# A routed-expert kernel: the table of slots holds whole token rows, so that an expert's rows come by one plain load

## The reference

```
gu = x @ shared_gate_up_w
shared = silu(gu[:, :512]) * gu[:, 512:] @ shared_down_w ; shared *= sigmoid(x @ shared_gate_w)
w, idx = top_k(softmax(x @ gate_w), 8) ; w /= sum(w)
pos  = running count of the tokens sent to this expert so far
slot = min(pos, 128)                       # capacity 128; later tokens are dropped
buf[expert, slot] = x[token]
out_e = (silu(buf @ gate_w[e]) * (buf @ up_w[e])) @ down_w[e]
y[token] += w * out_e[expert, slot]        # only where pos < 128
```

## Time and profile before

| What | Value |
|---|---|
| Median of three runs | 1972.29 us |
| The profiled execution's own time | 1962.54 us |
| Its span | 1960.8 us |
| PE busy | 1706.9 us (87%) |
| DVE busy | 1329.0 us (68%) |
| ACT busy | 971.5 us (50%) |
| POOL busy | 1068.3 us (54%) |
| DMA, mean over the span | 41 GB/s, 80.15 MB |
| Chain that ended last | PE 55%, issue 15%, DVE 14%, ACT 7%, POOL 4%, DMA 3% |

### The profile page before, as it was taken

The page is one execution under the profiler, slowest core; times in us unless marked ns, Lnnn a source line. Parts: engine busy times, 40 slices in busy tenths (PEclk is TensorE's granted clock), DMA queues, the critical chain, the costliest instruction groups (busy, mean ns, idle before and its releaser), DMA issues.

```text
span 1960.8 us, 51981 instructions
## 1 busy us (share of the span) xinstructions
PE 1706.9 (87%) x17309; PEld 1427.6 (73%) x17309; DVE 1329.0 (68%) x4615; ACT 971.5 (50%) x2803; POOL 1068.3 (54%) x1772
## 2 busy tenths in 40 slices
PE   3799999989899998999999999999999986457665
PEld 2687887878788887788878888888888864246554
DVE  5477777767677776677777777777777764335564
ACT  2365555555455554555555555555555543123332
POOL 2115555555455555555555555555555543568897
PEclk8899999999999999999999999999999997678999
DMA  4001100000000101000000000000000000147887
GB/s 126 8 14 21 21 19 19 19 14 19 19 19 19 19 19 19 19 19 19 17 16 19 19 19 19 19 19 19 19 19 19 18 13 13 45 124 186 199 205 154
DMA packets 97568, 80.15 MB, mean 41 GB/s; under 512 B 33835, under 2 KB 95224, under 8 KB 97528
## 3 DMA queue, kind: packets, MB, share of 16 engines
q1 hardware_dynamic: 68856, 60.46, 11.2%
q0 software_dynamic: 28672, 19.18, 5.5%
HBM read 51.63 MB, written 27.95 MB: 41 GB/s over the span
## 4 chain that ended last, share of the span: by engine, by line
PE 55%; issue 15%; DVE 14%; ACT 7%; POOL 4%; DMA 3%; another core or an unknown queue 1%; POOLq 0%; SPq 0%; DVEq 0%; ACTq 0%
PE bank L1055 15%; PE bank L964 7%; PE ps_m L964 5%; ACT p L787 3%; PE ps_lg L1113 3%; PE ps_yo L1069 3%; PE ps_lg L964 3%; PE ps_tr L986 3%; PE ps_yo L964 3%; PE ps_pt L1128 2%; PE bank L1041 2%; DMA xg<-xrows,gid 2%; PE ps_pt L964 1%; DVE rmax L1599 1%; PE ps_lg L1020 1%
## 5 line engine op out<-in xcount | busy, mean ns | idle before, releaser
L574 POOL DMA_INDIRECT table<-toki,slot x512 | 520.2, 1016 | 242.5 <-issue 196.3
L518 POOL TENSOR_TENSOR pool_pad<-pad_in 128x1 f32<-128x1 f32 x456 | 115.7, 254 | 400.8 <-PE ps_lg L1113 176.6
L787 ACT ACTIVATE p<-ps_lg,rmax 128x77 f32<-128x77 f32 x1024 | 235.6, 349 | 146.8 <-DVE rmax L1599 141.6
L1055 PE MATMUL bank<-h_h,wb 128*128 128x256 f16 x2048 | 266.3, 273 | 4.3 <-issue 2.2
L1055 PE MATMUL bank<-h_l,wb 128*128 128x256 f16 x2048 | 266.3, 273 | 0.0
L1055 PEld LDWEIGHTS bank<-h_l,wb 128*128 128x128 f16 x2048 | 200.8, 98 | 23.8 <-issue 0.2
L1055 PEld LDWEIGHTS bank<-h_h,wb 128*128 128x128 f16 x2048 | 193.2, 98 | 28.3 <-issue 2.8
L590 POOL TENSOR_TENSOR rs<-nt,minushalf 128x2 f32<-128x2 f32 x128 | 92.6, 724 | 188.2 <-DVE nt L1503 176.7
L1534 DVE SCALAR_TENSOR_TENSOR h_l<-bank,h_h 128x512 f16<-128x512 f32 x256 | 174.8, 683 | 12.0 <-ACT h_h L768 6.7
L1599 DVE TENSOR_REDUCE rmax<-ps_lg 128x8 f32<-128x616 f32 x128 | 101.6, 794 | 84.9 <-PE ps_lg L1113 84.8
L773 ACT ACTIVATE h_h<-bank 128x512 f16<-128x512 f32 x128 | 76.9, 601 | 124.3 <-PE bank L1055 124.3
(11 more groups left out here) (287 smaller groups left out, 4691.6 us busy)
## 6 DMA issues: line engine op xcount, KB each, us to landing
ew<-in_egu_w SPq DMA_DIRECT2D x64, 256.0 KB
xrows<-xr SPq DMA_DIRECT2D x32, 320.0 KB
x<-in_x SPq DMA_DIRECT2D x32, 256.0 KB
out<-x SPq DMA_DIRECT2D x32, 256.0 KB
table<-toki,slot POOLq DMA_INDIRECT x512
ew<-in_edown_w SPq DMA_DIRECT2D x64, 128.0 KB
ctx<-in_ctxT SPq DMA_DIRECT2D x32, 77.0 KB, 2.0
stage_b<-in_k SPq DMA_DIRECT2D x1, 1024.0 KB, 8.0
```

Source lines behind the costliest of these rows:

```text
L518: return g.tensor_tensor(pool_pad[:, site:site + 1], pad_in[:, :], pad_in[:, :], ALU.mult)
L574: g.indirect_dma_start(out=table, out_offset=bass.IndirectOffsetOnAxis(ap=slot[:, t, k:k + 1], axis=0), in_=toki[:, t:t + 1], in_offset=No ...
L787: ins = a.activation(p32[:, h * S2:(h + 1) * S2], ps_lg[:, h // HB, h % HB * S2:(h % HB + 1) * S2], ACT.Exp, bias=rmax[r % 2][:, h:h + 1])
L1055: ins = mm(two(bank[j % 2])[:, m % 2, :], wb1[:, k, m * P:(m + 1) * P], hp[:, k, :], start=(i == 0 and k == 0), stop=(i == 1 and k == FK - 1))
```

## The change

A table slot now holds a whole row of 321 float32 values (`TW`): the 320 of `xr` and the token's number. The array `xrows` is gone.

- **Batch loop.** In place of `store_rows`, SyncE copies `xr` to a second SBUF tile `xs` (`pass_rows`, 320 KB, SBUF to SBUF). That copy first waits until all scatters of the batches before have landed. VectorE writes the token's number into column 320 of `xs`. Each of the 16 scatters of a batch writes 128 rows of 1284 bytes from `xs` instead of 128 numbers of 4 bytes. Group "a" also waits for the copy.
- **Start.** The sentinel table of 32 KB is replaced by eight DMAs (`clear_table`), each of 1024 rows of 1284 bytes, 10.5 MB in all, placed behind `load_x(1)` in SyncE's order. GpSimd waits for them before its first scatter.
- **Between the loops.** Loading the table, its float copies, its transposition and `ids` are gone.
- **Expert loop.** SyncE loads an expert's 128 rows of the table with one plain DMA (`load_rows`), ahead of the expert's weights, four experts ahead. The gathers on GpSimd and the `gid` copies on VectorE are gone, with one of the two `plain`. `ids_across` is one float32 product of the last column of `xg` with the identity in place of two float16 products.

```diff
-            def store_rows(b):
+            def pass_rows(b):
                 sp.wait_ge(ch_ok, b + 1)
                 sp.wait_ge(ln_nm[3], b + 1)
-                sp.dma_start(xrows[bass.ds(b * S, S)].rearrange("(t p) n -> p t n", p=P), xr[:, :, :]).then_inc(xr_out, 16)
+                w(sp, scattered, 16 * T2 * TOPK * b)
+                sp.dma_start(xs[:, :, 0:XR], xr[:, :, :]).then_inc(xr_out, 16)
...
-            sp.wait_ge(consts, 1)
-            sp.dma_start(table.rearrange("(e c) o -> e (c o)", c=CAP), sent[:, :]).then_inc(table_dma, 16)
+            def clear_table(es):
+                sp.dma_start(table[es.start * CAP:es.stop * CAP].rearrange("(e c) n -> c e n", c=CAP),
+                             xg[1][:, :].unsqueeze(1).to_broadcast([P, len(es), TW])).then_inc(table_dma, 16)
...
             load_x(1)
+            for k in range(0, E, E // 8):
+                clear_table(range(k, k + E // 8))
             load_ctx(2)
             load_x(2)
...
-            def load_slots():
-                sp.wait_ge(scattered, 16 * T2 * TOPK * NB)
-                sp.dma_start(slots_row[:, :], table.rearrange("(e c) o -> e (c o)", c=CAP)).then_inc(table_dma, 16)
+            def load_rows(e, u):
+                w(sp, e_wt, e - XD + 1)
+                w(sp, e_aid, e - XD + 1)
+                w(sp, e_same, e - XD + 1)
+                sp.dma_start(xg[u][:, :], table[bass.ds(e * CAP, CAP)]).then_inc(e_x[u], 16)
+            def load_expert(e, u):
+                load_rows(e, u)
+                load_weights(e, u)
...
                 if group == "a":
                     pool.wait_ge(slots_ok, b + 1)
                     pool.wait_ge(tok_ok, b + 1)
+                    pool.wait_ge(xr_out, 16 * b + 16)
...
-                        in_=toki[:, t:t + 1], in_offset=None, bounds_check=NT - 1, oob_is_err=False,
+                        in_=xs[:, t, :], in_offset=None, bounds_check=NT - 1, oob_is_err=False,
...
-            def gather(e, u):
-                pool.wait_ge(e_gid, e + 1)
-                w(pool, e_tr, e - XD + 1)
-                w(pool, e_wt, e - XD + 1)
...
-                g.indirect_dma_start(
-                    out=xg[u][:, :], out_offset=None, in_=xrows,
-                    in_offset=bass.IndirectOffsetOnAxis(ap=gid[u][:, 0:1], axis=0),
-                    bounds_check=NT - 1, oob_is_err=False).then_inc(e_x[u], 16)
...
-                for half in (slots_h, slots_l):
-                    ins = mm(ps_row[:, 0:CAP], ident16[:, bass.ds(e, 1)].to_broadcast([P, P]), half[:, :],
-                             start=(half is slots_h), stop=(half is slots_l))
-                ins.then_inc(e_row, 1)
+                mm(ps_row[:, 0:CAP], xg[u][:, XR:TW].to_broadcast([P, P]), ident[:, :], start=True, stop=True).then_inc(e_row, 1)
```

More of the change, by code:

```diff
@@ L31 @@
 XR = D + E
+TW = XR + 1
 EPS = 1e-5
@@ L93, in build @@
 def build(nc, x, ctxT, maskT, g_xattn, g_ffn, wq0, wk0, wv0, bq0, bk0, bv0, k0, k1, k2, s0, s1, s2,
-          wqT1, wkvT1, wcT1, gates_w, sgu_w, sdown_w, egu_w, edown_w, out, xrows, table):
+          wqT1, wkvT1, wcT1, gates_w, sgu_w, sdown_w, egu_w, edown_w, out, table):
     es = ExitStack()
@@ L223, in build @@
         xr = sb("xr", [P, T2, XR])
+        xs = sb("xs", [P, T2, TW])
         th = sb("th", [P, IS // P, S])
@@ L245, in build @@
         x4 = sb("x4", [P, T2, D])
[L247 to L252, removed]
         aid = [sb(f"aid{i}", [P, 1], I32) for i in range(XD)]
-        xg = [sb(f"xg{i}", [P, XR]) for i in range(XD)]
+        xg = [sb(f"xg{i}", [P, TW]) for i in range(XD)]
         ew = [sb(f"ew{i}", [P, 3, D]) for i in range(XD)]
@@ L309, in build @@
         e_x, e_out = sems("e_x", XD), sems("e_out", 2)
-        ids_f, ids_t, e_gid, e_aid = (sem(n) for n in ("ids_f", "ids_t", "e_gid", "e_aid"))
+        e_aid = sem("e_aid")
         e_tr, e_eg, e_gu, e_th, e_ga, e_ac, e_dn, e_wt, e_y0 = (
@@ L433, in _ @@
             store_x4(0)
-            store_rows(0)
+            pass_rows(0)
             load_ctx(4)
@@ L438, in _ @@
                 store_x4(n - 2)
-                store_rows(n - 2)
+                pass_rows(n - 2)
                 load_ctx(n + 2)
@@ L443, in _ @@
                 store_x4(b)
-                store_rows(b)
-            store_rows(NB - 1)
+                pass_rows(b)
+            pass_rows(NB - 1)
             def load_weights(e, u):
@@ L458, in _ @@
             store_x4(NB - 1)
-            load_slots()
-            each_expert(sp, load_weights, XD)
+            sp.wait_ge(scattered, 16 * T2 * TOPK * NB)
+            for e in range(XD):
+                load_rows(e, e)
+            each_expert(sp, load_expert, XD)
             for par in range(2):
@@ L508, in _ @@
             for rows in xg:
-                g.memset(rows[:, :], 0.0).then_inc(consts2, 1)
+                g.memset(rows[:, 0:XR], 0.0).then_inc(consts2, 1)
+            g.memset(xg[1][:, XR:TW], float(NT)).then_inc(consts2, 1)
             g.memset(vc2[:, :, :], 0.0).then_inc(consts2, 1)
@@ L642, in _ @@
                 body(n)
-            pool.wait_ge(table_dma, 16 * 4)
+            pool.wait_ge(table_dma, 16 * 11)
             body(2)
@@ L683, in add_out @@
                     compute_op=ALU.add).then_inc(e_out[u % 2], 16)
-            g.memset(pool_pad[:, 3:5], 0.0).then_inc(pad_ok, 2)
-            for e in range(XD - 1):
-                gather(e, e)
+            g.memset(pool_pad[:, 4:5], 0.0).then_inc(pad_ok, 1)
             pool.wait_ge(x4_out, 16 * NB)
@@ L691, in step @@
                 if not isinstance(e, int):
-                    pool.wait_ge(pad_ok, 2 * (e - 2 * XD + 1))
-                if within(e, XD - 1):
-                    gather(e + XD - 1, (u - 1) % XD)
+                    pool.wait_ge(pad_ok, e - 2 * XD + 1)
                 if within(e, -1):
@@ L1337, in last_batch @@
                 d_dn(1, b)
-            pe.wait_ge(consts2, 30)
+            pe.wait_ge(consts2, 31)
             pe.wait_ge(setup_lo, 5)
@@ L1828, in _ @@
             from_bools(1)
-            dve.wait_ge(consts2, 30)
+            dve.wait_ge(consts2, 31)
             body(-1)
@@ L1865, in match @@
                 w(dve, e_cr, e - 2)
-                v.tensor_scalar(same[u % 2][:, :], ps_row[:, 0:CAP], idsf[:, bass.ds(e - 1, 1)], None, ALU.is_equal).then_inc(e_same, 1)
+                v.tensor_scalar(same[u % 2][:, :], ps_row[:, 0:CAP], xg[(u - 1) % XD][:, XR:TW], None, ALU.is_equal).then_inc(e_same, 1)
             def weight(e, u):
@@ L1905, in expert @@
                     summed(e - 1, (u - 1) % XD)
-            for e in range(XD - 1):
-                gather_ids(e, e)
             weight(0, 0)
@@ L1941 @@
     out = nc.dram_tensor("out_0", [NT + 3 * CAP, D], F32, kind="ExternalOutput").ap()
-    xrows = nc.dram_tensor("xrows", [NT, XR], F32, kind="Internal").ap()
-    table = nc.dram_tensor("table", [E * CAP, 1], I32, kind="Internal").ap()
-    build(nc, *args, out, xrows, table)
+    table = nc.dram_tensor("table", [E * CAP, TW], F32, kind="Internal").ap()
+    build(nc, *args, out, table)
     r = _run(nc, [arrays], core_ids=[0])
```

40 lines of the change are left out of this document (6 added, 34 removed).

## The result

Four runs of the changed kernel took 1904.17 to 1912.99 us, median 1907.7; four of the kernel before 1963.35 to 1974.40, median 1968.49. The ratio is 0.969 with a 95% interval of 0.965 to 0.973. That is faster, and faster than the forecast's whole range: 1949 was predicted, 1924 was the lower end. The profiled execution after took 1909.44 us with a span of 1907.5, against 1962.54 and 1960.8: 53.3 us less where 23 were predicted.

A forecast was written before the change was run, and what follows sets the result against it. POOL's queue was taken to set the expert step, with DMA the next bound; -21 in the expert loop and -1.8 between the loops gave -23 us, 1939.5 profiled, 1949 for the median, range 1924 to 1974.

The forecast's parts named there:

- Batch loop: "0, the gain side is 0 too": Batch loop: wait for scatters covered, dearer scatters vanish in POOL's idle half, store becomes equal copy; 0 us.
- Expert step: -21 us: Expert loop: step falls from 3.43 to 3.10 us over 63 steps, DMA the next bound; ends -36 and 0.
- POOL's ring: Expert loop before: add, `plain`, gather, second `plain` on POOL, closed at 3.42 us, sets the step.
- the divisor of 0.92: Expert loop: best DMA busy stretch is 92%, so 2.86 us of DMA an expert becomes 3.11.
- 2.34 from below, 3.43 from above: Expert loop: bounds on the step from adds, each waiting for the landing of the add two before.
- adds land 4.7 us late even alone: Expert loop: argument for the rival that the step stays, 3.25 us a step, total 1959; chance 0.13.
- The rival with 2.7 to 2.9 us: Expert loop: DMA freer than read, plain loads cheaper, adds don't stretch; -33 to -46 us, total 1930; chance 0.17.
- TensorE's own bound of 2.30 to 2.45: Expert loop: PE's work per expert, including the new float32 product, allows a step of 2.30 to 2.45 us.
- Between the loops: -1.8: Step into expert loop: one load replaces 7.2 us, less dearer scatters, their landing and the copy; ends -4 and +1.
- Scatter priced by the row: Rival: long-row scatters cost POOL as much as adds, 0.59 us more each; net +10 us, total 1982; chance 0.13.
- Out-of-bounds rows carried: Batch loop: out-of-bounds rows seem moved too, so 164 KB for each of 512 scatters, 84 MB; priced at 0.
- Start: 0: Start: clear of 10.5 MB takes 29 us, done before x(2) is needed; 0, upper bound +14 us.

The follow-up runs named there:

- x_thin: Changed kernel with scatters of 4 bytes a row into an array of their own, routing left out; 1856.35 us, ratio 0.982 to the kernel before.
- b_row runs: Kernel before, its scatters writing rows of 64, 512 or 1284 bytes into an array of their own, routing left out; ratios 0.989, 0.986, 0.988.
- e_deep: Changed kernel with adds in two DRAM arrays in turn, most waiting for the add four before; second array not added back; 1826.90 us, ratio 0.965.
- a_again: Changed kernel, unchanged, profiled a second time on another chip; 1845.27 us, ratio 0.976 to the kernel before.
- e_both: Changed kernel with adds in two DRAM arrays (second not added back) and down weights loaded for the first four experts only; 1880.18 us, ratio 0.958.

## Why the prediction was wrong

By its own steps, first those that decided.

- **Batch loop: "0, the gain side is 0 too".** This step failed, and with -18.4 us it is the largest miss. The forecast looked at what the new scatters cost beside the old ones and took the old ones as free of loss, because POOL has idle time in each batch. x_thin and the b_row runs show that 4-byte scatters disturb the loop and that rows from 64 bytes on don't. A scatter's own duration shows nothing of it: 969/996/1238 ns (min, median, max) against 967/993/1236 in the earlier trace rows. The trace of before had the signs: a scatter with 8.53 us of idle time "<-issue" ahead of it, waits of 5 us that end by "remote", and batches of 50 to 57 us where others take 49.05. How a short scatter delays the engines stays open. The forecast read two neighbouring batches and never listed all of them.
- **Expert step: -21 us, taken at 3.10 us; it is 2.87, -35.7.** Half of the mechanism was right: POOL's ring is gone and DMA is nearly full. So was the work: 0.975 of 2.87 us is 2.80 us of DMA an expert, forecast 2.86. Two things failed, the divisor of 0.92, the best stretch of before, and the choice of DMA as what sets the step. That share belonged to a stretch that POOL's ring held up, so it said nothing of what the engines reach; they reach 0.98 here and 1.02 in e_deep. The step is set by the adds' chain, which the forecast bounded (2.34 from below, 3.43 from above) and passed over. Its 4.67 us run from one add's start to another's, so "adds land 4.7 us late even alone" took too much for the landing: by a_again a landing takes 3.8 us alone and 5.4 beside the loads, and 0.8 to 0.9 more pass before the next add. The rival with 2.7 to 2.9 us had the step that came, but its reason ("adds don't stretch") was wrong: they stretch by 1.6 us. TensorE's own bound of 2.30 to 2.45 was a little high; e_both has steps of 2.20.
- **Between the loops: -1.8, measured -4.8.** The 16 scatters did not get dearer (first to last issue 19.2 us as before, forecast +1.0), and their landing shows no extra time: the load is issued 1.14 us after the last scatter's end, as before (forecast +1.0). The load takes 2.4 us (1705.82 to 1708.23; 2.9 taken). The copy cost 0.6 (forecast 0.5): group "a" starts 1.37 us after the slots are there, before 0.77.
- **Scatter priced by the row (chance 0.13): false.** The mean is 1.016 us in both kernels. What makes the add cost POOL 1.55 us is not the length of its rows.
- **Out-of-bounds rows carried: false.** The total went from 80.15 to 101.10 MB, 21 MB more: the clear's 10.5 and 8192 rows of 1284 bytes, 10.5. The constant 512 bytes a scatter that the earlier trace rows show are the queue's own. The profile's counter of bytes written to HBM, 27.95 before and 111.84 MB after, counts the other rows as if written; queues and rates don't. It changed nothing in the sum.
- **Start: 0, measured +1.6** (the first store of x4 at 141.96 against 140.40). The clear is hidden.
- **The end: +5.5 us, not foreseen.** Before, the adds kept pace with POOL. Now the chain of adds lags behind TensorE, and after the last transposes it is worked off: POOL issues the last add at 1900.74, 11.9 us after them.

The Trainium skill's rule in the forecast ("DMA: Bandwidth & Descriptors", Rules for kernel authors), that moving a DMA to another engine brings issue time but no bandwidth, holds as far as the runs go: the gain was issue time on POOL. The forecast then let a share of 83% stand for a limit of bandwidth, which the rate shows false: 203 GB/s before, 233 after, 253 in e_deep. The estimate from its other section, 10 to 15% dearer rows of 1284 bytes, doesn't show in 2.80 us an expert against 2.86 before; but a gather became a plain load at the same time, so the price of the row alone stays unmeasured.

## What to carry to other kernels

A busy share measured while something else sets the pace is no ceiling: divide by it only after the waits show the resource itself waited for. Where DMAs wait for each other's landing, price the chain, landing time plus what passes until the next start, over depth, at the load that the change will bring. And before calling a loop's change zero, list the length of every iteration of the old loop: iterations that differ without a reason are time that a change can give back.

## What the hardware showed that was not expected

- Indirect scatters of 128 rows into DRAM cost the batch loop more with rows of 4 bytes than with rows of 64: over 448 of them 28 us (1401.0 and 1372.7, traces of two sets), and within one set 21 us of the whole kernel (medians 1962.38 and 1941.16). Against rows of 1284 bytes it is 15 us within a set (1343.8 and 1328.8). Each scatter takes POOL the same 1.0 us. Some 5 us are one stall, ahead of the 114th scatter (8.5 us against 3.0). The rest goes with waits that end by "remote", 31, 8 and 7 us of engine time over the 28 batches in the three traces with 4-byte rows and none in the other eleven, and is spread over many batches. Why was not settled.
- Ahead of the 114th, 227th, 340th and 453rd scatter, so every 113 (509.94, 857.50, 1207.53, 1556.23 us in the changed kernel), POOL stops for 2.7 to 3.7 us with nothing to wait for in the profile, in all fourteen traces; only the first stop is longer with 4-byte rows.
- A scatter's price on POOL doesn't depend on the length of the rows from 4 to 1284 bytes (mean 1.016 us in both kernels), nor on how many are in bounds (1.021 us for the first 128 scatters of the changed kernel, 1.014 for the others, when nearly all slots are full).
- An accumulating DMA of 128 rows of 1 KB lands 3.8 us after its start with little beside it and 5.4 us beside 224 GB/s (a_again). With the 0.8 us up to the next one, a chain two deep gives at best one every 2.3 and some 2.9 to 3.1 us.
